# Two layers of cross attention and experts on one core: half of the routed tiles get a fixed owner, and the order of all steps is written anew

## What is computed

```python
x = x + L0_xattn(layernorm(x), ctx)      # 16 heads of 8, softmax over 512 keys
x = x + L0_ffn(layernorm(x))             # 8 experts 128-512-128, exact GELU, top 1
x = x + L1_xattn(layernorm(x), ctx)      # 16 query heads, 8 key heads, rounded inputs and ternary weights
x = x + L1_ffn(layernorm(x))             # 15 experts 128-128-128 and one shared, ReLU, top 3
```

```python
logits = (x @ w_red) @ wg_n.T
gates = softmax(logits); idx = argmax(gates); scores = gates[idx]
h = gelu(x @ w1[e] + b1[e]); y = h @ w2[e] + b2[e]
out = y[idx] * scores
```

## Time and profile before

| | |
|---|---|
| median of 3 runs | 331.83 us (322.08 to 334.65) |
| profiled execution, its own time | 324.32 us |
| its span, first to last instruction | 322.2 us |
| TensorE / VectorE / ScalarE / GpSimd busy | 249.1 / 169.4 / 131.9 / 94.2 us |
| mean granted TensorE clock | 0.799 of full speed |

### The profile page before, as it was taken

How to read it: one execution, slowest core, us unless ns; L and a number is a source line. 1 busy time by engine, 2 the same in 40 slices (tenths; PEclk the granted TensorE clock), 3 DMA queues, 4 the chain that set the end, 5 groups by cost and what they waited for, 6 DMA issues and landing times.

```text
span 322.2 us, 5008 instructions
## 1 busy us (share of the span) xinstructions
PE 249.1 (77%) x1731; PEld 115.5 (36%) x1731; DVE 169.4 (53%) x489; ACT 131.9 (41%) x287; POOL 94.2 (29%) x154
## 2 busy tenths in 40 slices
PE   2446789989986789992489899956798884379995
PEld 1241433231432233370332343511122333267874
DVE  7636875864861400026733453471778705667564
ACT  4310355654673352121231167563067381145452
POOL 6950970162800194403081431420000102210000
PEclk9965767985997799997575856995579598589999
DMA  5280163040440000000100000621000000000000
GB/s 157 18 214 11 35 167 83 0 132 1 144 146 10 1 0 2 0 2 1 41 8 2 0 3 0 187 77 43 8 0 2 0 2 0 0 1 3 16 2 16
DMA packets 12680, 12.37 MB, mean 38 GB/s; under 512 B 2658, under 2 KB 11064, under 8 KB 12656
## 3 DMA queue, kind: packets, MB, share of 16 engines
q0 software_dynamic: 2400, 6.58, 7.5%
q1 hardware_dynamic: 8816, 4.95, 5.6%
q10 hardware_dynamic: 1440, 0.53, 0.7%
HBM read 7.80 MB, written 0.26 MB: 25 GB/s over the span
## 4 chain that ended last, share of the span: by engine, by line
PE 54%; DVE 21%; ACT 6%; issue 5%; DMA 5%; SPq 4%; POOL 4%; POOLq 1%; DVEq 0%; ACTq 0%
DVE mx L941 10%; PE OB L1309 7%; PE SA L1277 6%; PE X L1405 5%; PE SB L1294 4%; DMA Q<-nm 3%; PE X L1400 3%; PE X L1423 3%; ACT prob L710 3%; PE SB L1471 2%; PE X L1382 2%; SPq L424 2%; DMA K<-kp 2%; SPq L507 2%; PE X L1235 2%
## 5 line engine op out<-in xcount | busy, mean ns | idle before, releaser
L941 DVE TENSOR_REDUCE mx<-SA 128x1 bf16<-128x512 f32 x128 | 81.4, 684 | 52.8 <-PE SA L1277 51.6
L710 ACT ACTIVATE prob<-SB 128x512 f32<-128x512 f32 x128 | 68.7, 596 | 41.6 <-PE SB L1294 41.3
L1277 PE MATMUL SA<-K,Q 64*128 64x512 bf16 x128 | 46.4, 478 | 20.0 <-DVE mx L941 11.5
L1309 PE MATMUL OB<-prob,V 128*32 128x256 f32 x512 | 47.2, 450 | 2.6 <-ACT oT L718 2.4
L631 POOL COPY wq<-w0s 128x1024 f32 x32 | 31.8, 1040 | 27.8 <-PE X L1423 24.2
L1294 PE MATMUL SB<-Q,K 64*128 64x256 bf16 x256 | 35.7, 318 | 4.7 <-DMA Q<-nm 3.1
L1277 PEld LDWEIGHTS SA<-K,Q 64*128 64x128 bf16 x128 | 10.1, 99 | 59.0 <-DVE mx L941 41.0
L551 POOL TENSOR_SCALAR vareps<-mv 128x2 f32<-128x2 f32 x10 | 1.9, 192 | 77.0 <-DVE mv L840 76.7
L1294 PEld LDWEIGHTS SB<-Q,K 64*128 64x128 bf16 x256 | 12.1, 101 | 27.8 <-issue 12.7
L1309 PEld LDWEIGHTS OB<-prob,V 128*32 128x32 f32 x512 | 11.4, 116 | 19.9 <-issue 15.3
L1405 PE MATMUL X<-wq,xs 128*32 128x512 f32 x64 | 16.8, 775 | 0.6 <-POOL wq L631 0.6
(11 more groups left out here) (293 smaller groups left out, 376.7 us busy)
## 6 DMA issues: line engine op xcount, KB each, us to landing
w0s<-in_L_ffn_w_dram POOLq DMA_DIRECT2D x16, 256.0 KB, 4.1
wq<-in_L_ffn_eW_dram POOLq DMA_DIRECT2D x2, 960.0 KB, 7.2
K<-kp SPq DMA_DIRECT2D x12, 128.0 KB, 2.6
Q<-qp SPq DMA_DIRECT2D x18, 64.0 KB, 2.0
Q<-nm SPq DMA_DIRECT2D x64, 0.5 KB
K<-kp SPq DMA_DIRECT2D x12, 64.0 KB, 2.1
cx<-in_ctx_dram SPq DMA_DIRECT2D x2, 256.0 KB, 3.5
Q<-qp ACTq DMA_DIRECT2D x6, 64.0 KB, 4.2
```

The source lines that it names most:

```text
L710: act.activation(prob[:, g % 2, 2 * (i % 2) + a, 2 * u:2 * u + 2, :].rearrange("p k q -> p (k q)"), SB[n % NSB][:, :], ACT.Exp).then_inc(s ...
L941: dve.tensor_reduce(mx[:, g % 2, i // 2, r, a:a + 1], SA[n % NSA][:, :], AX, ALU.max, negate=True).then_inc(s_sa_max, 1)
L1277: pe.matmul(SA[u % NSA][:, :], Q[rows, b, p, r:NQ:R], K[n][b][rows, key_group(n, p), :], start=True, stop=True).then_inc(s_sa_full, 1)
L1309: last = pe.matmul(OB[32 * j:32 * j + 32, 0:NQ], V[n][:, b, kt, first:first + 32], prob[:, gg % 2, j, kt, :], start=(kt == 0), stop=(kt == ...
```

## The change

Every expert now owns one fixed tile: tile e belongs to expert e for e = 0 to 7. The tokens of an expert beyond its first 32 go to the tiles 8 to 15 (`MOVED` = 8), which are given out as before. So chunks 0 and 1 take their weights straight from `w0s` (`chosen_weights`), `owners` of these tiles is constant and made once by GpSimd, and only `weights0` (b, 2) and (b, 3) remain. `slots0` now makes, for each token and expert, its rank within the expert, its place if it is among the first 32, and the distance by which it moves if it isn't; `h0` waits for the expert loads itself, where GpSimd did. `eid` is released by the copy that writes it, without a second copy behind it.

`SCHEDULE` is a new order of the steps, with 16 copies fewer. Among its differences: of batch 1, `stats` f0 to `slots0` stand inside the experts of batch 0; `gather0` (1) and all of batch 1's `h0` stand between `scatter0` (0) and `scores` (8, 0) or just behind; all `h0` come before the first `exp` of layer 1; the chain of `o1` and `f1` of batch 0 stands inside the last attention groups and that of batch 1 inside the experts of batch 0; `kstack` (1, 0) and (1, 1) come behind `max_rows` 7 and 9; `load_expert` 3, 2 and 1 come ahead of the first scores; `bias1` (1) is the last step but the store. `s_ctxT` becomes one semaphore for each batch, and the memset of `mx` comes first on VectorE with a semaphore of its own. The file grows, so lines from 45 on shift.

```diff
@@ -42,6 +42,7 @@
 TILE = 32
 CHUNKS = 4
 TILES = 4 * CHUNKS
+MOVED = TILES - E0
 SLOTS = TILES * TILE
 NSA, NSB = 2, 3
...
-SCHEDULE = [('zeros', 1), ('ctx_turn', 0), ('load_small', 2), ('values_ones', 0), ('zeros', 0), ('stats', 'q0', 0),
...
-    ('slots0', 0), ('tiles0', 0), ('values', 7, 1), ('gather0', 0), ('values', 7, 2), ('permT0', 0, 0),
-    ('values', 7, 3), ('permT0', 0, 1), ('weights0', 0, 0), ('weights0', 0, 1), ('h0', 0, 0), ('gelT0', 0, 0),
-    ('h0', 0, 1), ('y0', 0, 0), ('weights0', 0, 2), ('gelT0', 0, 1), ('h0', 0, 2), ('y0', 0, 1),
-    ('weights0', 0, 3), ('gelT0', 0, 2), ('h0', 0, 3), ('out_turn', 0, 1, 0), ('y0', 0, 2), ('out_turn', 0, 1, 1),
-    ('gelT0', 0, 3), ('att_turn', 0, 1), ('y0', 0, 3), ('out_proj', 0, 1), ('scatter0', 0), ('stats', 'f0', 1),
-    ('stats', 'q1', 0), ('norm', 'f0', 1), ('norm', 'q1', 0), ('turn', 'f0', 1), ('quant', 'q1', 0), ('red0', 1),
-    ('turn', 'q1', 0), ('logits0', 1), ('qproj', 1, 0), ('gate_exp0', 1), ('qstack', 1, 0), ('count0', 1),
-    ('slots0', 1), ('tiles0', 1), ('gather0', 1), ('permT0', 1, 0), ('permT0', 1, 1), ('scores', 8, 0),
...
+SCHEDULE = [('zeros', 0), ('constants',), ('stats', 'q0', 0), ('ctx_measure',), ('norm', 'q0', 0), ('w0_turn', 0),
+    ('stats', 'q0', 1), ('ctx_turn', 0), ('load_small', 3), ('ctx_turn', 1), ('load_expert', 3), ('keys_ones', 0),
+    ('zeros', 1), ('turn', 'q0', 0), ('w0_turn', 1), ('qproj', 0, 0), ('load_small', 1), ('kproj', 0, 0),
+    ('load_expert', 2), ('qstack', 0, 0), ('load_bo',), ('w1_measure',), ('kstack', 0, 0), ('load_expert', 1),
+    ('norm', 'q0', 1), ('kproj', 0, 1), ('values_ones', 0), ('vproj', 0, 0), ('scores', 0, 0), ('scores', 0, 1),
+    ('scores', 0, 2), ('scores', 0, 3), ('scores', 1, 0), ('max_rows', 0), ('w1_quant',), ('turn', 'q0', 1),
+    ('scores', 1, 1), ('scores', 1, 2), ('scores', 1, 3), ('load_small', 2), ('load_small', 0), ('load_expert', 0),
+    ('w1_turn',), ('kstack', 0, 1), ('scores', 2, 0), ('exp', 0, 0), ('max_rows', 1), ('ctx_quant',),
...
+    ('permT0', 0, 0), ('gather0', 0), ('values', 7, 0), ('exp', 7, 2), ('tiles0', 0), ('weights0', 0, 2),
+    ('permT0', 0, 1), ('gate_exp0', 0), ('exp', 7, 3), ('h0', 0, 0), ('h0', 0, 1), ('values', 7, 1),
+    ('values', 7, 2), ('gelT0', 0, 0), ('weights0', 0, 3), ('values', 7, 3), ('gelT0', 0, 1),
+    ('out_turn', 0, 1, 0), ('out_turn', 0, 1, 1), ('h0', 0, 2), ('h0', 0, 3), ('att_turn', 0, 1),
+    ('out_proj', 0, 1), ('y0', 0, 0), ('gelT0', 0, 2), ('stats', 'f0', 1), ('y0', 0, 1), ('norm', 'f0', 1),
+    ('turn', 'f0', 1), ('gelT0', 0, 3), ('red0', 1), ('logits0', 1), ('y0', 0, 2), ('y0', 0, 3), ('count0', 1),
+    ('slots0', 1), ('scatter0', 0), ('gather0', 1), ('stats', 'q1', 0), ('norm', 'q1', 0), ('h0', 1, 0),
+    ('tiles0', 1), ('gelT0', 1, 0), ('h0', 1, 1), ('quant', 'q1', 0), ('weights0', 1, 2), ('turn', 'q1', 0),
+    ('qproj', 1, 0), ('qstack', 1, 0), ('y0', 1, 0), ('h0', 1, 2), ('gelT0', 1, 1), ('weights0', 1, 3),
...
+    ('y0', 1, 2), ('scores', 9, 1), ('y0', 1, 3), ('scores', 9, 2), ('gate_exp0', 1), ('scatter0', 1),
+    ('stats', 'q1', 1), ('scores', 9, 3), ('exp', 8, 0), ('exp', 8, 1), ('norm', 'q1', 1), ('exp', 8, 2),
+    ('scores', 10, 0), ('vproj', 1, 0), ('values', 8, 0), ('exp', 8, 3), ('max_rows', 9), ('quant', 'q1', 1),
+    ('scores', 10, 1), ('values', 8, 1), ('kstack', 1, 1), ('scores', 10, 2), ('turn', 'q1', 1), ('exp', 9, 0),
+    ('scores', 10, 3), ('qproj', 1, 1), ('qstack', 1, 1), ('scores', 11, 0), ('max_rows', 10), ('exp', 9, 1),
...
+    ('out_turn', 1, 1, 0), ('out_turn', 1, 1, 1), ('hidden1', 0, 0), ('hidden1', 0, 1), ('hidden1', 0, 2),
+    ('stats', 'o1', 1), ('hidden1', 0, 3), ('norm', 'o1', 1), ('output1', 0, 0), ('hidden1', 0, 4),
+    ('output1', 0, 1), ('output1', 0, 2), ('hidden1', 0, 5), ('hidden1', 0, 6), ('output1', 0, 3),
+    ('hidden1', 0, 7), ('output1', 0, 4), ('hidden1', 0, 8), ('output1', 0, 5), ('quant', 'o1', 1),
+    ('hidden1', 0, 9), ('output1', 0, 6), ('hidden1', 0, 10), ('output1', 0, 7), ('output1', 0, 8),
+    ('hidden1', 0, 11), ('hidden1', 0, 12), ('output1', 0, 9), ('att_turn', 1, 1), ('output1', 0, 10),
+    ('out_proj', 1, 1), ('stats', 'f1', 1), ('hidden1', 0, 13), ('hidden1', 0, 14), ('bias1', 0),
+    ('norm', 'f1', 1), ('output1', 0, 11), ('hidden1', 0, 15), ('output1', 0, 12), ('output1', 0, 13),
...
+    ('output1', 1, 14), ('output1', 1, 15), ('bias1', 1), ('store', 1)]
...
@@ -391,6 +397,10 @@
         def columns(stage, b):
 
             return hT[:, b, :] if stage[0] != "q" else hT[:, b, :].rearrange("d (p r) -> d p r", r=R)
+
+        def chosen_weights(c, j):
+
+            return w0s[:, 4 * c + j, :] if 4 * c < E0 else wq[:, c % 2, j, :]
 
         def buffer_free(engine, step):
...
+            pool.tensor_copy(first_at[:, :, :], places[0:1, 0:TILE * E0:TILE].unsqueeze(1).broadcast_to([1, R, E0])).then_inc(s_place, 1)
+            pool.tensor_scalar(move_by[:, :], places[0:1, 0:TILE * E0:TILE], -1.0, float(TILE * (E0 - 1)), ALU.mult, ALU.add).then_inc(s_place, 1)
+            then(pool.memset(owners[:, 0:E0, :], 1.0))
+            then(pool.affine_select(out=owners[:, 0:E0, :], in_=owners[:, 0:E0, :], compare_op=ALU.is_equal, fill=0.0, base=0,
+                                    pattern=[[1, E0], [0, TILE]], channel_multiplier=-1))
+            pool.memset(owners[:, E0:TILES, :], 0.0).then_inc(s_place, 1)
...
                                                   QSCALE if n == 0 else 1.0, ALU.mult, ALU.mult)
                     last.then_inc(s_wtern, 1)
                 elif kind == "slots0":
-                    pool.wait_ge(s_slot, 2 * nth(*step))
-                    if step[1]:
-                        pool.wait_ge(*xfull(("y0", step[1] - 1, CHUNKS - 1)))
-                    pool.tensor_copy(owners[:, :, :], owner[:, :].unsqueeze(2).broadcast_to([E0, TILES, TILE])).then_inc(s_owner, 1)
+                    b = step[1]
+                    pool.wait_ge(s_owner, nth(*step))
+                    if b:
+                        pool.wait_ge(*xfull(("y0", b - 1, CHUNKS - 1)))
+                    pool.tensor_copy(owners[:, E0:TILES, :], owner[:, :].unsqueeze(2).broadcast_to([E0, MOVED, TILE])).then_inc(s_owners, 1)
                 elif kind == "weights0":
                     _, b, c = step
-                    if c == 0:
-                        pool.wait_ge(s_eid, b + 1)
-                    if (b, c) == (0, 0):
+                    pool.wait_ge(*xread("tiles0", b))
+                    if b == 0:
                         pool.wait_ge(in_f0, 16 * 2 * E0)
-                    before = nth(*step) - 3
-                    if before >= 0:
-                        pool.wait_ge(*xfull(("y0", before // CHUNKS, before % CHUNKS)))
+                    else:
+                        pool.wait_ge(*xfull(("y0", b - 1, c)))
                     for j in range(4):
-                        place = pool.value_load(eid[0:1, b, 4 * c + j:4 * c + j + 1], min_val=0, max_val=E0 - 1)
+                        place = pool.value_load(eid[0:1, b, 4 * c + j - E0:4 * c + j - E0 + 1], min_val=0, max_val=E0 - 1)
                         pool.tensor_copy(wq[:, c % 2, j, :], w0s[:, bass.ds(place, 1), :].rearrange("p o f -> p (o f)")).then_inc(s_wq, 1)
                 elif kind == "wg_norm":
                     pool.wait_ge(s_wgsq, 1)
...
+            dve.memset(mx[:, :, :, :, :].rearrange("p g x r c -> p (g x r c)").bitcast(F32), 0.0).then_inc(s_mx, 1)
...
+                    if i == 0 and g == 0:
+                        dve.wait_ge(s_mx, 1)
+                    if i == 0 and g >= 2:
+                        dve.wait_ge(s_nm, nth("max_rows", g - 2))
...
+                    bank = xbank(step)
+                        dve.wait_ge(*xfull(("gather0", b - 1)))
+                        dve.wait_ge(s_owners, b)
-                        dve.wait_ge(s_owner, b)
-                    then(dve.tensor_scalar(past[:, :], places[0:E0, 0:TILES], xbank(step)[0:E0, 16:17], None, ALU.is_ge))
-                    dve.scalar_tensor_tensor(owner[:, :], places[0:E0, 0:TILES], xbank(step)[0:E0, 17:18], past[:, :],
-                                             ALU.is_ge, ALU.subtract).then_inc(s_slot, 1)
-                    for r in range(R):
-                        last = dve.tensor_tensor_reduce(junk8[:, r, :], xbank(step)[:, r * E0:(r + 1) * E0], oh0[:, b, r, :], 1.0, 0.0,
+                    rank = bank[:, 0:R * E0].rearrange("p (r e) -> p r e", r=R)
+                    place = bank[:, R * E0:2 * R * E0].rearrange("p (r e) -> p r e", r=R)
+                    move = bank[:, 2 * R * E0:2 * R * E0 + E0].unsqueeze(1).broadcast_to([P, R, E0])
+                    dve.tensor_copy(moves[:, :, :], move)
+                    then(dve.tensor_scalar(past[:, :], places[0:E0, 0:MOVED], bank[0:E0, 40:41], None, ALU.is_ge))
+                    then(dve.scalar_tensor_tensor(late[:, :, :], rank, float(TILE), moves[:, :, :], ALU.is_ge, ALU.mult))
```

(43 more changed lines are left out.)

128 lines of the change are left out of this document (60 added, 68 removed), and 25 rows, old and new, of the table SCHEDULE.

## The result

The kernel after takes 263.49 us (median of 4 executions, 260.42 to 265.76), the kernel before 326.95 beside it (321.52 to 334.65). The ratio is 0.816, 95% interval 0.803 to 0.829. I had said 294 with a range of 279 to 312. Stages are compared in the profiled executions; 1 or 2 us in a stage decide nothing.

The account below looks back on a forecast made before the run. TensorE, busy 249.1 of 322.2 us, was the engine to fill, with three serial-chain holes and a 0.799 clock. Terms: 36.8 us won, 3.2 paid, 33.6 off 324.3 gives 290.7; with scatter 294, range 279 to 312.

Parts of the forecast that it names:

- third chain: Hole from 266.9 to 281.4 us: moved into attention groups and below batch 0's experts; 8 of 9.4 us idle won.
- SyncE's queue: Layer 1's key issues, moved behind max_rows 7 and 9, no longer delay the last maxima before exp; 2.5 us won.
- Copies: Batch 0's expert chunks 2 and 3 no longer wait for GpSimd weight copies; 6.3 us won, batch 1 nothing.
- Slots: Three more small VectorE instructions each time in slots0; 1.0 us paid for both batches.
- First and second chain: Holes at 144 to 161 and 209 to 226.6 us filled with other work; 9 and 7 us won.
- End: bias1 (1) as last step, no longer partly hidden in the loop before; 1.2 us paid.
- Clock: Batch 1's expert matmul groups, three of four chunks slow, run earlier in dense work; 4 us won, bounds 0 and 8.
- Rival B: The clock rises more in both layers' attention; 10 to 12 us more won, 280 to 282 us, chance 0.11.
- Start: Before first scores: projections fill the key stack wait, but three expert loads precede it; taken 0, bounds -3 and +3 us.
- Signs: Expected in the profile: TensorE busy about 240 us, no 14 us window under 70% after the start, three table loads.
- Rival A: Holes move instead of closing, as chains among scores delay VectorE's reductions; 306 us, 309 with scatter, chance 0.17.
- Rivals C and D: C: half clock through both attention stages, 336 us, chance 0.04. D: an unread wait eats all, within 2% of 332, 0.05.

Follow-up runs that it names:

- e1: Kernel after's code with fixed owners, but the steps in the old order without the 16 copies; 316.96 us, ratio 0.965 to the kernel before.
- e2: Kernel after with all 32 weight copies made again and h0 of chunks 2 and 3 behind y0 of chunks 0 and 1; 291.76 us.
- e4: Fixed owners, old step order up to the gather of batch 0, the new order from there; 283.59 us.
- m1: e8 with the bias of batch 1 moved into the last output loop instead of last; 260.25 us, ratio 0.791.
- e5: Kernel before with only layer 1's two key stacks moved later, behind max_rows 7 and scores 8; 325.78 us beside 330.21.
- k1: Kernel after with the router's chain of batch 0 put back behind the last row maxima of layer 0; 267.68 us, ratio 0.819.
- k2: Kernel after with batch 1's key, query and first value projections put back among the scores of group 1; 271.93 us, ratio 0.833.
- k3: Kernel after with scores seven steps ahead of exp in layer 0 instead of mostly 8 to 11; 275.29 us, ratio 0.835.
- e10: e1 with layer 0's scores and row maxima four steps earlier from the 11th scores step on; 316.03 us, ratio 0.960.
- k4: e1 with the steps before the first exp as in the new list and batch 0's router chain four to six exp steps earlier; 322.31 us.
- e6: Kernel before, nothing moved, with unread filler matmuls in 19 places where TensorE waited; 318.22 us, ratio 0.977.
- e8: Kernel after with loads of experts 3, 2 and 1 moved behind the first scores; 257.77 us, ratio 0.775.
- m2: m1 with six filler matmuls ahead of the turn of layer 1's first queries; 252.13 us, ratio 0.771.

## Why the prediction was wrong

The direction and the mechanism (chains laid beside other work) were right; the size was not, by 27 us of span. Two steps failed: the third chain, mis-sized by 10 us, and SyncE's queue, all that I had for layer 0's attention, which shortened by 22. By my own steps:

- *Copies*, 6.3 us: measured 6.4 in S2 (e1). Right, batch 1's copies at nothing too. All groups of eight take 1.06 or 1.94 us now. But this holds for the old order; in the new one the copies would have cost about 25 (e2). My sum adds the parts as if each had one price. With owners alone the span is 6.6 us shorter, with the order alone (e2) 32.0, with both 60.5: 22 us come only where both are there.
- *Slots*, 1.0 paid: VectorE's chain from the first slot instruction to the permutation is 1.28 us long for 0.90, so 0.8 for both batches. Right.
- *First and second chain*, 9 and 7, with the clock's 4 and 1 paid for the projection: S3 and S4 together are 18.9 us shorter, where these terms less the slots made 18. Right as a sum, in part by luck. Part by part it is not: S3 grew by 3.2 us since the experts of batch 1 moved into it, and its wait of 2.8 us remained.
- *Third chain*, 8: this step failed. I counted the idle 9.4 us of the hole and took less. S5 became 17.0 us shorter (e4 shows the same 17.0 beside e1). What left it was the whole stretch of 14.5 us: its 5.1 us of turns and projections, at clock 0.65, moved into S4 and into the expert loop too. The loop itself lost the other 2.5. S5's idle time fell from 15.5 to 5.05 us and its busy time by 6.6. A hole is as long as it is, not as long as the idle time in it.
- *End*, 1.2 paid: wrong in sign. m1 took the cost away and the stage became 0.6 us longer.
- *SyncE's queue*, 2.5: this is the step that failed most, since it was all that I had for S1. By itself it was not far off (e5: 4.4, with a scatter as large), but S1 shortened by 22.3. I had looked for long stretches with TensorE little busy, and S1 had one only at its end: it had 14 us of idle time, in waits of 0.2 to 3 us, and half-clock stretches between them. Three things in the order carry it, each 6.5 to 7.8 us when taken out alone (k1, k2, k3): the keys of batch 1 made ahead of the scores, the router's chain begun before the scores end, and scores 8 to 11 steps ahead of exp. The last alone (e10) and the first two together (k4) brought nothing in the old order; that the missing one then takes over as the wait fits k4's view (5.0 us for Q<-nm, 2.5 in e1), but is not shown for each.
- *Clock*, 4: I took it from batch 1's groups of eight, three of four slow. Two of four still are (1.94 us at 138.15 and 143.06), so of this source about 1.8 came.
- *Rival B* (the clock rises more): it rose from 0.799 to 0.902, and B's 280 would have been nearer. As the reason for S1 it falls: e6 has 0.886 in the order of before and won 6.6 us of 322. For S4 it holds in part, with the 5 us estimated above. The rule that I set against the clock's gain, from "TensorE: Matmul & The Clock Gate" of the Trainium skill, section "A second HAM failure mode: psum-queue depth-cycling", isn't borne out in layer 0: from 43.7 to 91.7 us scores, exp and values cycle through their banks at a granted clock of 1.00 in each window of 8 us. In layer 1's attention the clock did change between its two levels (0.87 over S4), and no run says why.
- *Tables*, 0 on the path: three loads, as read off the steps, of 1.28 us each, and no wait of TensorE leads to one.
- *Start*, 0 with bounds of 3: 2.0 us later, and for the reason named (e8), which was worth 4.5.
- *Signs*: TensorE is busy 218 us, not 240, and one window of 14 us is under 70% (118.7 to 132.7, 68%, around the wait in S3); the others held.
- *Rival A* (the holes move) is seen in S3, whose wait stayed, and in k4. *Rivals C and D*: no sign (C's 156.6 is 156.1 by its own factors); TensorE's waits for VectorE in front of scores fell from 11.5 us to 7.0.

What the runs leave open: how the 22 us of S1 divide, as its parts work only together; what the clock gave in S4; the 5 us by which spans and times differ for e1; and S2's low clock in k3.

## What to carry to other kernels

Before costing a reordering, ask of every stage, holes or not, how full the engines are whose instructions don't stretch with the clock: in S1 TensorE showed 84% and looked full, VectorE showed 65%, and the order brought VectorE to 84%. Where several chains are nearly critical, undo one at a time in the good version; added one at a time to the bad version they showed nothing here. And parts of a change that free each other can't be priced apart. A filler paid where TensorE had a queue of its own behind the wait (m2, 4.2 us for one place); 19 of them among the chains of other engines (e6) shortened the span by 6.6.

## What the hardware showed that I had not expected

- A VectorE instruction of 0.36 us on two SBUF tiles took 8.23 beside GpSimd copies, to the end of the ninth. VectorE's row maxima, which read PSUM, were not held: in the kernel before six of them took 3.88 us from 166.71 on, beside copies that ran until 170.00.
- Expert loads of 0.5 MB each on GpSimd's queue held up a stack of keys on SyncE's: from its first issue to the first scores 13.05 us with three loads ahead, 8.45 with these three behind the scores, 9.93 in the kernel before with one ahead.
- A wait of 2.82 us, which ended at 131.40, was followed by half clock: groups of eight took 1.94 us at 138.15 and still at 143.06. Six filler matmuls in it kept the clock at 1.00 for the whole stage (m2).
